# A graph network with experts on one Trainium2 core: 12 dense tiles in four blocks of three where there were 13 in five, and 50 edge pairs where there were 46

## What is computed

```python
def _gat(x, src, dst, W, a_src, a_dst, b, heads, ch, concat):
    n = x.shape[0]
    h = (x @ W).reshape(n, heads, ch)
    es = (h * a_src).sum(-1)
    ed = (h * a_dst).sum(-1)
    e = jax.nn.leaky_relu(es[src] + ed[dst], SLOPE)
    m = jax.ops.segment_max(e, dst, num_segments=n)
    w = jnp.exp(e - m[dst])
    den = jax.ops.segment_sum(w, dst, num_segments=n)
    alpha = w / den[dst]
    msg = h[src] * alpha[:, :, None]
    out = jax.ops.segment_sum(msg, dst, num_segments=n)
    out = out.reshape(n, heads * ch) if concat else out.mean(axis=1)
    return out + b
...
    h = _gat(x, src, dst, W1, a1_src, a1_dst, b1, HEADS, HID, True)
    h = jax.nn.relu(_layernorm(h, ln_g, ln_b))
    out = _gat(h, src, dst, W2, a2_src, a2_dst, b2, 1, D_OUT, False)
...
    x = x + _L0_gnn_ref(_layernorm(x, axis=-1), edge_index, ...)
    x = x + _L0_ffn_ref(_layernorm(x, axis=-1)[None], ...)[0]
```

## Time and profile before

| | us |
|---|---|
| median of 3 runs | 1572.9 |
| lowest, highest | 1552.66, 1572.95 |
| the profiled execution | 1562.67 |
| its span, first to last instruction | 1560.7 |
| up to the first dense step of layer 1 | 103 |
| first block of layer 1, one tile wide | 52 |
| rest of layer 1's dense steps | 478 |
| between the layers | 31 |
| layer 2 up to the last logits | 404 |
| choice of experts, experts, output | 484 |

### The profile page before, as it was taken

The page is one execution under the profiler, slowest core; times in us unless marked ns, Lnnn a source line. Parts: engine busy times, 40 slices in busy tenths (PEclk is TensorE's granted clock), DMA queues, the critical chain, the costliest instruction groups (busy, mean ns, idle before and its releaser), DMA issues.

```text
span 1560.7 us, 21436 instructions
## 1 busy us (share of the span) xinstructions
PE 1259.3 (81%) x6282; PEld 959.0 (61%) x6283; DVE 915.4 (59%) x2551; ACT 725.5 (46%) x1834; POOL 692.8 (44%) x626
## 2 busy tenths in 40 slices
PE   0767798979889989749778788873699999999990
PEld 0545354535445545337567577652699999999980
DVE  6769898999899987525555665667511111111115
ACT  0357665657656667425444544442034344335330
POOL 3600788656666671056565666520422222222220
PEclk9979899999999999869898999886699999999995
DMA  7012633623633470243443554422022222121116
GB/s 223 5 42 78 166 91 89 179 75 89 176 87 89 125 198 25 96 126 102 150 144 103 155 158 113 136 56 78 11 91 94 94 94 91 37 94 37 36 31 250
DMA packets 120379, 160.59 MB, mean 103 GB/s; under 512 B 53198, under 2 KB 93009, under 8 KB 120302
## 3 DMA queue, kind: packets, MB, share of 16 engines
q0 software_dynamic: 28384, 76.23, 17.9%
q1 hardware_dynamic: 86608, 78.89, 16.2%
q10 hardware_dynamic: 5310, 4.58, 0.9%
HBM read 124.98 MB, written 34.64 MB: 102 GB/s over the span
## 4 chain that ended last, share of the span: by engine, by line
PE 50%; DVE 26%; issue 8%; ACT 5%; DMA 4%; another core or an unknown queue 4%; ACTq 1%; SPq 1%; POOL 1%; DVEq 0%; POOLq 0%
PE bank L1381 13%; PE bank L1389 12%; PE bank L1263 9%; PE bank L1214 6%; DVE ring_a L1805 5%; PE bank L1335 4%; DVE ohk L1546 3%; ACT ring_a L1062 2%; DVE ohs L1543 2%; DVE st L1468 2%; PE bank L1123 1%; PE bank L1146 1%; DVE hit L1710 1%; PE bank L1246 1%
## 5 line engine op out<-in xcount | busy, mean ns | idle before, releaser
L750 POOL DMA_INDIRECT arena<-rows,idx_e x385 | 432.8, 1124 | 291.7 <-PE bank L1214 106.4
L1263 PE MATMUL bank<-ring_a,slots 128*65 128x384 f32 (+1 forms) x1000 | 343.9, 457 | 51.7 <-DVE ring_a L1805 45.0
L1335 PE MATMUL bank<-h2t,ring_a 128*128 128x257 f32 x650 | 186.2, 425 | 82.3 <-DVE ring_a L1880 59.3
L982 ACT ACTIVATE ring_a<-vbb,slots 128x384 f32<-128x384 f32 (+1 forms) x500 | 243.8, 562 | 15.4 <-DMA vbb<-v_rows 12.2
L1263 PEld LDWEIGHTS bank<-ring_a,slots 128*65 128x65 f32 x1000 | 136.1, 142 | 181.8 <-issue 101.2
L1805 DVE SCALAR_TENSOR_TENSOR ring_a<-ring_a,arena 128x1536 f32<-128x1536 f32 (+1 forms) x125 | 192.3, 1540 | 16.4 <-ACT ring_a L982 10.3
L1086 ACT ACTIVATE ring_a<-bank,cols 128x128 f32<-128x128 f32 x432 | 128.2, 370 | 158.0 <-PE bank L1381 157.2
L1335 PEld LDWEIGHTS bank<-h2t,ring_a 128*128 128x128 f32 x650 | 126.9, 207 | 116.3 <-DVE ring_a L1880 68.4
L1214 PE MATMUL bank<-arena,ring_a 128*128 128x257 f32 (+1 forms) x770 | 194.3, 402 | 0.0
L1214 PEld LDWEIGHTS bank<-arena,ring_a 128*128 128x128 f32 x770 | 157.4, 205 | 34.9 <-issue 5.4
L1880 DVE SCALAR_TENSOR_TENSOR ring_a<-ring_a,p,arena 128x256 f32<-128x256 f32 (+1 forms) x175 | 79.3, 464 | 114.9 <-ACT ring_a L1062 84.4
(11 more groups left out here) (277 smaller groups left out, 1721.9 us busy)
## 6 DMA issues: line engine op xcount, KB each, us to landing
counts_all<-arena SPq DMA_DIRECT2D x13, 800.0 KB
arena<-counts_all SPq DMA_DIRECT2D x13, 800.0 KB
arena<-in_L_ffn_W SPq DMA_DIRECT2D x8, 1024.0 KB, 7.5
arena<-rows,idx_e POOLq DMA_INDIRECT x385
arena<-ytab SPq DMA_DIRECT2D x4, 1280.0 KB, 11.0
XB<-general_sums SPq DMA_DIRECT2D x38, 130.0 KB
vbb<-in_L_ffn_W SPq DMA_DIRECT2D x4, 1024.0 KB
spare<-in_L_ffn_W SPq DMA_DIRECT2D x4, 1024.0 KB
```

The source lines that it names most:

```text
L750: pool.indirect_dma_start(to[:, k, 0:width], None, table, bass.IndirectOffsetOnAxis(idx_e[:, m * PAIR + k:m * PAIR + k + 1], 0)).then_inc( ...
L982: ins = act.activation(S1[q % SLOTS1][:, h * k * P:(h + 1) * k * P].rearrange("p (t n) -> p t n", n=P), vb1[:, 0:k, h, :], ACT.Copy, scale ...
L1263: pe.matmul(bank[h][0:CH + 1, 0:w_], slots[:, s, h * (CH + 1):(h + 1) * (CH + 1)], S1[q % SLOTS1][:, h * w_:(h + 1) * w_], start=(s == 0), ...
L1335: ins = pe.matmul(bank[(j % 2) * 2 + i][:, 0:W2T], S2[q2 % SLOTS2][:, i * P:(i + 1) * P], h2t[:, s, 0:W2T], start=(s == 0), stop=(s == NT ...
```

## The change

`ND` is 12, so tile 12 goes to the edge tiles. The 12 dense tiles make four blocks of three, the first of them wide as well: 100 steps instead of 125 in layer 1, and six blocks of two, 150 steps instead of 175, in layer 2. The pairs become 50, in steps 27 to 95 of layer 1 (28 to 112 before) and 3 to 135 of layer 2 (3 to 159). The first group of one-hots holds 72 visits instead of 24. The planner gets a later end for an edge group of a single tile, and some buffers move: the count buffers of layer 2 swap places, and `vbb` grows by 128 columns.

```diff
-ND = 13
+ND = 12
 DW = ND * PER_TILE
-B1 = ((0, 1),) + tuple((t, min(3, ND - t)) for t in range(1, ND, 3))
+B1 = tuple((t, min(3, ND - t)) for t in range(0, ND, 3))
 B2 = tuple((t, min(2, ND - t)) for t in range(0, ND, 2))
 Q1, Q2 = len(B1) * NT, len(B2) * NT
...
-PAIR1 = [28 + p * 86 // PAIRS for p in range(PAIRS)]
-PAIR2 = [3 + p * 160 // PAIRS for p in range(PAIRS)]
+PAIR1 = [27 + p * 70 // PAIRS for p in range(PAIRS)]
+PAIR2 = [3 + p * (Q2 - 15) // PAIRS for p in range(PAIRS)]
...
-USES = [("window", w) for w in windows_of(0)]
+USES = [("window", w) for t in range(B1[0][0], B1[0][0] + B1[0][1]) for w in windows_of(t)]
...
-        groups.append(Group(tl, False, PAIR1[last_pair(tl[-1])]))
+        groups.append(Group(tl, False, PAIR1[last_pair(tl[-1])] + 8 * (2 - len(tl))))
...
-        vbb = sb("vbb", [P, max(4096, 2560 + PAIR * T1W)])
+        vbb = sb("vbb", [P, max(4224, 2560 + PAIR * T1W)])
...
-        C2 = [arena_u[:, a:a + 6400].rearrange("p (t h n) -> p t h n", t=2, h=NT) for a in (9600, 0)]
+        C2 = [arena_u[:, a:a + 6400].rearrange("p (t h n) -> p t h n", t=2, h=NT) for a in (0, 9600)]
...
-        fw1 = [vbb[:, 2048:4096].rearrange("p (k n) -> p k n", k=2), arena[:, 5248:7296].rearrange("p (k n) -> p k n", k=2)]
+        fw1 = [vbb[:, 2176:4224].rearrange("p (k n) -> p k n", k=2), arena[:, 5248:7296].rearrange("p (k n) -> p k n", k=2)]
```

## The result

The changed kernel took 1601.8 us against 1566.2 in the same session: ratio 1.0267 (95% interval 1.0214 to 1.0320), slower. The forecast was 1565, no change; the time lies 6 us outside the range. The profiled execution took 1601.2 (span 1599.5).

What follows compares the result with a forecast made beforehand. TensorE and VectorE bound layer 1 with GpSimd close behind; a chain of waits bounds layer 2. Against the profiled 1562.67 us, -4 + 4 - 3 = -3 gave 1559.7, set to 1565 us (no change), range 1538 to 1596.

Steps and rivals of the forecast that it cites:

- (d): Boundary behind block 0: three count stores ahead of the v rows delay block 1, +5 us, between 0 and 8.74.
- (e): Rest of layer 1: GpSimd's 250 gathers at 1.64 us decide; dense part ends at 638 against 642, -4 us.
- (g): Layer 2 to the last logits: fewer steps against 7 more pairs, tiles closed inside and table loads, -3 us.
- (a): Ahead of layer 1: 72 one-hot visits instead of 24 before the dense loop, +16.4 us, all exposed.
- (b): Ahead of the first dense step: spreading v for three tiles instead of one, +5.4 us.
- (f): Tail of layer 1: two more edge tiles project behind the last dense step, +4 us, from 0 to 8.
- (c): Block 0 of layer 1, three tiles wide: VectorE's steps take 3.18 us instead of 2.12, +26.5 us.
- rival B: Layer 1: gathers at 1.435 us plus 0.3, engines stand behind late pairs, +21, 1589 us; chance 0.23.
- A: Rival: GpSimd keeps pace in layer 1, dense part ends at 622, 1549 us; chance 0.22.
- rival C: Layer 2 takes the new pairs and loads into its waits, -35, 1533 us; chance 0.10.
- rival B with all loads exposed: Slower layer-1 gathers plus all of layer 2's table loads exposed, 13 us more: 1602 us.
- nothing is full: Layer 2 before the change: no engine over 77% busy, time a chain in which engines wait for one another.

Runs made afterwards that it cites:

- three_of_five: Changed kernel with only 3 of the 5 row gathers of each layer-1 pair from the fourth pair on: 1496.8 us, ratio 0.9985.
- no_loads: Changed kernel with the exponentials of layer 2's pairs replaced by Relu, so some 50 table loads go: 1603.2 us, ratio 1.0287.
- runs_paused_b: Changed kernel, last 20 edge-run gathers held until 12 node tiles are projected, the last 10 until 22; a repeat run: ratio 1.0207.
- before_again: Kernel before, nothing changed, run again for a second profile: 1499.9 us, ratio 1.0000.
- before_slots3_b: Kernel before with 3 slots instead of 4 for gathered pairs in layer 2, a repeat run: ratio 1.0012.

## Why the prediction was wrong

**The sum failed in three terms, (d), (e) and (g), and the two large ones are GpSimd's.** At 1500, where no wait without a cause blurs the stages, (a), +16.4, and (b), +5.4, are right to 2 us: +20.0 measured. (f) is right, 5.5 for 4. (c), 25 x 1.06 = 26.5, is right too, +27.0 from the first multiply's start to the last one's end, in steps of 3.18 us.

(d), taken as 5 between 0 and 8.7, is 10.6 (last multiply's end to block 1: 8.6 to 19.2). I had bounded it by the stores alone; the load that SP issues between them and the destination terms, 5.2 us when it stands behind three stores, was in the order that I quoted and not in my sum.

(e) fails in "plus 5 us in which three slots are full and the first pair isn't summed". Its other parts stand: the first gather at 200.1 (forecast 200.4), a gather 1.298 + 0.30 = 1.60 us (forecast 1.64). But the 250 took 436 us, not 415: 14 us of standing at the start instead of 5, and some 22 us more of waiting for slots whose pair was summed late, less 10 for the cheaper gathers. I summed GpSimd as if the two engines that it feeds never held it up, and them as if it never did. Here three engines were within 10% of each other and waited for one another's slots, and both waits occurred. That is rival B's end (1.74 us from gather to gather, layer 1 past 655), reached by waits and not by dearer gathers. GpSimd did wait for TensorE by tens of us, which I had named as A's sign; A is refuted all the same, by three_of_five: to keep pace GpSimd would have had to save 37 us.

(g), -3, is +13.1 at 1500. The step that failed is "7 pairs x 2.4", and the loads: I priced a pair at TensorE's 2.4 us. A pair costs GpSimd 5 x 1.27 = 6.4 us, which I had written down only against rival C ("250 gathers x 1.28 = 320 in the some 350 us up to step 135") and did not take as the bound itself. It is one: 318.3 us of gathers without a stop, then 43 us from the last gather to the last logits. The 7.7 us of exposed table loads are nearly nothing (no_loads: 4 us for all 50, at 1560).

**The session of the result was the other kind**, and there the stages miss in part elsewhere. Layer 1 behind block 0 came out much as at 1500 (-46.0 against a forecast of -57.3), so (e) failed there too. But the largest single miss is ahead of the first dense step, +38.5 for +21.8, and 13.7 us of it is the wait without a cause that runs_paused_b took away; (g) missed by 9.4 us, and what made that is open. That 1601.8 falls on the 1602 of rival B with all loads exposed is chance: the gathers cost 1.28 us there and not 1.44, and the loads weren't exposed. The forecast had given 0.15 to more than 2% slower, for these loads or for "engines that wait for one another worse than I sum"; the second is what happened in layer 1.

**What misled me was the profile that I read.** In it 62 us of waits without a cause lay in layer 2, GpSimd stood there as long, and "nothing is full" was read off windows that held them. The page said "another core or an unknown queue 4%" for a kernel on one core. I read past that row. Without those waits layer 2 of the same kernel (before_again, 676:1018) shows GpSimd at 222 us busy with 226 gaps of 0.3 us, 289 of 342.

## What to carry to other kernels

Add to every engine's busy time the gap that stands between two of its instructions before calling a stage unbound: 0.95 us of gather and 0.30 of issue are 1.25, and 5 of them per pair bounded layer 2 of the changed kernel at 1500, where the engine is 76% busy by its windows (235.93 of 310 us in 695:1005). Where a change moves work from dense steps to gathered pairs, price the pair on the engine that issues it, from the first moment at which it may start to the last, standing included. And when the chain gives a share to an unknown cause, take a second profile before working out differences of a few per cent from the first, and when such a wait seems gone, look whether it stands under another name.

## What was not expected of the hardware

One kernel on one chip ran at 1500 us in one session and at 1561 in another, with the same work; the difference lay in layer 2 (403.4 us against 342.5), in waits without a recorded cause; of the 20 over 3 us in the two first profiles, 17 ended 0.6 to 3.5 us after GpSimd paused. The long ones occurred in streams of gathers 1.23 to 1.27 us apart (edge runs of the changed kernel, layer 2). In the 45 us stream of edge runs of the kernel before, whose gathers stand 1.42 us apart, there was none over 2.3 us, and none in layer 1 at 1.6 us. At 1500 a stream of 318 us had none. Breaking or shortening a stream removed or shortened the wait at that place (runs_paused_b: 13.7 us to none; before_slots3_b: 14.9 to 8.2). No loading of code shows there: the DMA records of the first profile of the changed kernel show no block of instructions between 26.9 and 77.2 us, where the wait of 13.7 us lies. What in the chip is held meanwhile, and why only in some sessions, stays open.

The duration of a gather hardly depends on its rows: 0.92 us for 96 or 50 partitions of edge runs, 0.95 for 128 of layer 1's rows.
